# Scores on half the array's rows in banks shared with q, and the norm's factors by transposes

## The reference

```
scores = q @ k.T * 32**-0.5 + slope[h] * (j - i), masked to j <= i
out = softmax(scores) @ v; x = x + out @ Wout.T
```

```
qh = softmax over the head's 64 columns of Wq q; kh = softmax over the 1024 positions of Wk k
out = Wo (context(kh, vh) applied to qh) + bo
out = out / max(sqrt(sum over the 128 channels of out*out), 1e-12) * g * sqrt(128); x = x + out
```

## Time and profile before

| | us |
|---|---|
| median of three runs (lowest, highest) | 3303.05 (3302.89, 3307.04) |
| span of the profiled execution | 3299.9 |
| PE busy in the span | 3128.8 (95%) |
| DVE busy | 1773.3 (54%) |
| ACT busy | 1045.8 (32%) |
| POOL busy | 507.1 (15%) |

### The profile page before, as it was taken

How to read it: one execution, slowest core, us unless ns; L and a number is a source line. 1 busy time by engine, 2 the same in 40 slices (tenths; PEclk the granted TensorE clock), 3 DMA queues, 4 the chain that set the end, 5 groups by cost and what they waited for, 6 DMA issues and landing times. The chain is left out here.

```text
span 3299.9 us, 41826 instructions
## 1 busy us (share of the span) xinstructions
PE 3128.8 (95%) x15136; PEld 2393.9 (73%) x15136; DVE 1773.3 (54%) x2927; ACT 1045.8 (32%) x2356; POOL 507.1 (15%) x525
## 2 busy tenths in 40 slices
PE   7999997799999999999996799999999899999998
PEld 6888886566666666666663688888887788888887
DVE  5311112466666666666663655555555655555555
ACT  2100000566665566666651211111111211111111
POOL 2100000233333333333332100000000100000000
PEclk9999999899999999999996899999999999999999
DMA  4222223111111111111110432222122521231222
GB/s 144 93 73 75 73 70 116 41 39 38 43 46 51 38 38 39 50 38 51 38 33 31 129 82 55 76 65 75 54 82 76 153 64 54 81 81 54 62 74 78
DMA packets 83350, 218.73 MB, mean 66 GB/s; under 512 B 11984, under 2 KB 18256, under 8 KB 81232
## 3 DMA queue, kind: packets, MB, share of 16 engines
q1 hardware_dynamic: 83280, 217.78, 21.8%
HBM read 175.79 MB, written 41.94 MB: 66 GB/s over the span
## 5 line engine op out<-in xcount | busy, mean ns | idle before, releaser
L312 PE MATMUL ff_ps<-h_xT_hi,w_hi 128*128 128x512 f32 x1376 | 538.2, 391 | 13.2 <-DVE h_xT_lo L96 13.2
L312 PE MATMUL ff_ps<-h_xT_lo,w_hi 128*128 128x512 f32 x1376 | 537.1, 390 | 0.0
L312 PE MATMUL ff_ps<-h_xT_hi,w_lo 128*128 128x512 f32 x1376 | 537.0, 390 | 0.0
L1042 ACT ACTIVATE w_hi<-words 128x1024 fp32r<-128x1024 f32 x134 | 142.5, 1063 | 697.3 <-DVE words L1087 697.3
L1127 DVE TENSOR_TENSOR acc<-ff_po,acc 128x512 f32<-128x512 f32 x352 | 243.0, 692 | 210.6 <-PE ff_po L312 209.9
L312 PE MATMUL qkv_acc<-w_hi,xT_hi 128*128 128x512 f32 x768 | 300.9, 392 | 9.2 <-DVE w_lo L255 9.2
L312 PEld LDWEIGHTS ff_ps<-h_xT_hi,w_hi 128*128 128x128 f32 x1376 | 259.5, 189 | 68.3 <-issue 8.8
L312 PE MATMUL qkv_acc<-w_hi,xT_lo 128*128 128x512 f32 x768 | 299.4, 390 | 0.0
L312 PE MATMUL qkv_acc<-w_lo,xT_hi 128*128 128x512 f32 x768 | 299.3, 390 | 0.0
L312 PEld LDWEIGHTS ff_ps<-h_xT_hi,w_lo 128*128 128x128 f32 x1376 | 259.4, 189 | 54.1
L312 PEld LDWEIGHTS ff_ps<-h_xT_lo,w_hi 128*128 128x128 f32 x1376 | 259.6, 189 | 53.8
(11 more groups left out here) (156 smaller groups left out, 5305.9 us busy)
## 6 DMA issues: line engine op xcount, KB each, us to landing
words<-in_w SPq DMA_DIRECT2D x90, 512.0 KB, 3.5
qkv<-qkv_out SPq DMA_DIRECT2D x96, 256.0 KB, 2.0
words<-in_w SPq DMA_DIRECT2D x176, 128.0 KB, 4.0
sc<-in_s SPq DMA_DIRECT2D x88, 256.0 KB, 4.3
qk_in<-qkv SPq DMA_DIRECT2D x16, 1024.0 KB, 4.9
w_stage<-in_w_attn SPq DMA_DIRECT2D x56, 256.0 KB, 3.0
qkv_rows<-in_x SPq DMA_DIRECT2D x16, 512.0 KB, 3.8
ctx_in<-in_context SPq DMA_DIRECT2D x16, 512.0 KB, 3.7
```

The lines of the kernel that those rows point to most:

```text
L312: last = nc.tensor.matmul(out, left, right, start=n == 0, stop=n == len(pairs) - 1)
L1042: nc.scalar.activation(dst, src, ACT.Copy).then_inc(s["split_hi"], 1)
```

## The change

- The scores of a head group are two products of 64 rows and 256 columns: rows 0 to 63 hold heads 0 and 1, rows 64 to 127 heads 2 and 3. `kD` shrinks to two key blocks of 128 columns. The two results lie in two banks of PSUM, the first half of each bank of `pair_s`. DVE biases both with one instruction.
- `bank_s` and `bank_q` give way to `pair_s`: q is its bank 0, where half of the scores lie too; y is formed in both banks.
- PE's order in a step becomes s, P, AV, q, k, kt, m, d. s waits for q tile t-3 to be read, q for the scores of the same step to be biased.
- m tiles 2 and 3 go into `pair_k`; the third waits for all four copies of kT.
- The norm: each column of eight factors, repeated 128 times by a stride of nothing, is transposed into `bank_p` and `bank_d`. `diag`, its instruction and POOL's wait for it go.

```diff
-    kD = sb("kD", [P, G, HG, P], F32, ph)
+    kD = sb("kD", [P, G, 2, P], F32, ph)
...
+    pair_s = pb("pair_s", [P, 2, N], ph)
+    half_s = pair_s[:, :, 0:2 * P]
+    bank_q = pair_s[:, 0, :]
...
+    y_banks = [pair_s[:, e, :] for e in range(2)]
+    norm_banks = [bank_p, bank_d]
...
-    m_room = [pair_o[:, D - P:D]] * 2 + [bank_s[:, 0:P]] * 2
+    m_room = [pair_o[:, D - P:D]] * 2 + [pair_k[:, N:N + P], pair_k[:, 0:P]]
...
-            last = nc.vector.tensor_copy(kD[at, :, j, :], qkT[at, 1, :, :])
+            last = nc.vector.tensor_copy(kD[at, :, j % 2, :], qkT[at, 1, :, :])
...
+        by_half = [v.rearrange("p (a j) s -> p a (j s)", a=2) for v in (sc[:, t % SR, :, :],
+                                                                       bias[:, t * HG:(t + 1) * HG, :])]
+        nc.vector.scalar_tensor_tensor(by_half[0], half_s, float(HD) ** -0.5, by_half[1], ALU.mult, ALU.add).then_inc(
...
+            if own and t < G:
+                if t == 0:
+                    pe.wait_ge(s["a_out"], 2 * b + 2)
+                    pe.wait_ge(s["kd_out"], b + 1)
+                elif cross and t > 2:
+                    pe.wait_ge(s["q_subbed"], c * KT + t - 2)
+                else:
+                    pe.wait_ge(s["s_biased"], b * G + t)
+                for e in range(2):
+                    at = slice(e * 2 * HD, (e + 1) * 2 * HD)
+                    last = nc.tensor.matmul(half_s[:, e, :], qkT[at, 0, t, :], flat(kD[at, t, :, :]), start=True,
+                                            stop=True)
+                last.then_inc(s["s_done"], 1)
...
+            n = t - 2
+            if cross and 0 <= n < KT:
+                if n % 4 == 0:
+                    pe.wait_ge(s["x1_norm"], 2 * c + n // 4 + 1)
+                if own and t < G:
+                    pe.wait_ge(s["s_biased"], b * G + t + 1)
+                elif n:
+                    pe.wait_ge(s["q_subbed"], c * KT + n)
+                else:
+                    pe.wait_ge(s["y_scaled"], b)
+                nc.tensor.matmul(bank_q, xn[:, n * P:(n + 1) * P], wq_sb[:, 0, :], start=True,
+                                 stop=True).then_inc(s["q_done"], 1)
...
                 if i == 2:
-                    pe.wait_ge(s["s_biased"], (b + 1) * G)
+                    pe.wait_ge(s["kt_out"], (b + 1) * XT)
...
-            pe.wait_ge(s["n_diag"], c + 1)
-            for e, bank in enumerate(norm_banks):
-                last = nc.tensor.matmul(bank, ones[:, :], flat(diag[:, 4 * e:4 * e + 4, :]), start=True, stop=True)
+            pe.wait_ge(s["n_pow"], c + 1)
+            for k in range(KT):
+                last = nc.tensor.transpose(norm_banks[k // 4][:, k % 4, :],
+                                           n_sq[:, 1, k:k + 1].to_broadcast([P, P]), ident[:, :])
...
-            if cross:
-                pool.wait_ge(s["r_done"], b + 1)
...
-            dve.wait_ge(s["n_pow"], c + 1)
-            nc.vector.tensor_tensor(diag[:, :, :], ident[:, :].unsqueeze(1).to_broadcast([P, KT, P]),
-                                    n_sq[:, 1, :].unsqueeze(2).to_broadcast([P, KT, P]), ALU.mult).then_inc(s["n_diag"], 1)
```

More of the change, by code:

```diff
@@ L370, in attention_phase @@
     y_sq = kE
-    diag = xn[:, :].rearrange("p (a b) -> p a b", a=KT)
     n_sq = sb("n_sq", [P, 2, KT], F32, ph)
     neg8 = sb("neg8", [P, KT], F32, ph)
-    bank_s = pb("bank_s", [P, N], ph)
-    bank_q = pb("bank_q", [P, N], ph)
+    pair_s = pb("pair_s", [P, 2, N], ph)
+    half_s = pair_s[:, :, 0:2 * P]
+    bank_q = pair_s[:, 0, :]
     bank_p = pb("bank_p", [P, HG, P], ph)
@@ L380, in attention_phase @@
     pair_k = pb("pair_k", [P, 2 * N], ph)
-    norm_banks = [bank_q[:, :], flat(bank_d[:, :, :])]
-    turn4 = [bank_s[:, :].rearrange("p (a b) -> p a b", a=4), bank_q[:, :].rearrange("p (a b) -> p a b", a=4),
-             bank_p[:, :, :], bank_d[:, :, :]]
+    y_banks = [pair_s[:, e, :] for e in range(2)]
+    norm_banks = [bank_p, bank_d]
+    turn4 = [b.rearrange("p (a b) -> p a b", a=4) for b in y_banks] + [bank_p[:, :, :], bank_d[:, :, :]]
     names = ("qk_loaded v_loaded x_loaded ctx_loaded stored setup_in distances powers filled slopes masked gain w_in0 w_in1 w_in2 w_in3 w_hi_done w_lo_done "
@@ L390, in attention_phase @@
              "x_done x1_done x1_stats x1_aggr x1_mom x1_rstd x1_norm copied "
-             "y_done y_out y_squared y_gained n_done n_clamped n_pow n_diag r_done y_scaled fin").split()
+             "y_done y_out y_squared y_gained n_done n_clamped n_pow r_done y_scaled fin").split()
     s = {n: sem("a_" + n) for n in names}
@@ L480, in bias_scores @@
         dve.wait_ge(s["s_done"], b * G + t + 1)
-        nc.vector.scalar_tensor_tensor(flat(sc[:, t % SR, :, :]), bank_s[:, :], float(HD) ** -0.5,
-                                       flat(bias[:, t * HG:(t + 1) * HG, :]), ALU.mult, ALU.add).then_inc(
+        by_half = [v.rearrange("p (a j) s -> p a (j s)", a=2) for v in (sc[:, t % SR, :, :],
+                                                                       bias[:, t * HG:(t + 1) * HG, :])]
+        nc.vector.scalar_tensor_tensor(by_half[0], half_s, float(HD) ** -0.5, by_half[1], ALU.mult, ALU.add).then_inc(
             s["s_biased"], 1)
@@ L517, in turn_tensor @@
                     pe.wait_ge(s["p_out"], b * G + n)
+                elif cross:
+                    pe.wait_ge(s["y_scaled"], b)
                 for j in range(HG):
@@ L520, in turn_tensor @@
                 last.then_inc(s["p_done"], 1)
[L521 to L538, removed]
             n = t - 3
@@ L542, in turn_tensor @@
                     pe.wait_ge(s["v_loaded"], (b + 1) * 16)
+                    if cross:
+                        pe.wait_ge(s["x1_done"], 2 * b)
                 if n == G // 2:
@@ L570, in turn_tensor @@
                 if i == 2:
-                    pe.wait_ge(s["s_biased"], (b + 1) * G)
-                elif i:
+                    pe.wait_ge(s["kt_out"], (b + 1) * XT)
+                elif i == 1:
                     pe.wait_ge(s["m_out"], b * XT + i)
@@ L599, in turn_tensor @@
             pe.wait_ge(s["d_out"], (c + 1) * KT)
-            if own:
-                pe.wait_ge(s["s_biased"], (b + 1) * G)
-            for e, bank in enumerate((bank_s, bank_q)):
+            pe.wait_ge(s["q_subbed"], (c + 1) * KT)
+            for e, bank in enumerate(y_banks):
                 for j in range(XT):
-                    last = nc.tensor.matmul(bank[:, :], z[:, j, :], qT[:, j, e * N:(e + 1) * N], start=j == 0,
+                    last = nc.tensor.matmul(bank, z[:, j, :], qT[:, j, e * N:(e + 1) * N], start=j == 0,
                                             stop=j == XT - 1)
@@ L679, in turn_scalar @@
             act.wait_ge(s["y_done"], c + 1)
-            for e, bank in enumerate((bank_s, bank_q)):
-                last = nc.scalar.activation(y[:, e * N:(e + 1) * N], bank[:, :], ACT.Identity, bias=bo_sb[:, 0:1])
+            for e, bank in enumerate(y_banks):
+                last = nc.scalar.activation(y[:, e * N:(e + 1) * N], bank, ACT.Identity, bias=bo_sb[:, 0:1])
             last.then_inc(s["y_out"], 1)
@@ L748, in turn_vector @@
                 dve.wait_ge(s["q_done"], c * KT + n + 1)
-                nc.vector.tensor_reduce(q_max[:, n, :], bank_q[:, :].rearrange("p (h d) -> p h d", d=XD), AX.X,
+                nc.vector.tensor_reduce(q_max[:, n, :], bank_q.rearrange("p (h d) -> p h d", d=XD), AX.X,
                                         ALU.max).then_inc(s["q_maxed"], 1)
@@ L752, in turn_vector @@
                 nc.vector.tensor_tensor(qr[:, n % SR, :].rearrange("p (h d) -> p h d", d=XD),
-                                        bank_q[:, :].rearrange("p (h d) -> p h d", d=XD),
+                                        bank_q.rearrange("p (h d) -> p h d", d=XD),
                                         q_max[:, n, :].unsqueeze(2).to_broadcast([P, 8, XD]),
@@ L820, in turn_vector @@
             for e, bank in enumerate(norm_banks):
-                last = nc.vector.tensor_tensor(y[:, e * N:(e + 1) * N], y[:, e * N:(e + 1) * N], bank, ALU.mult)
+                last = nc.vector.tensor_tensor(y[:, e * N:(e + 1) * N], y[:, e * N:(e + 1) * N], flat(bank[:, :, :]), ALU.mult)
             last.then_inc(s["y_scaled"], 1)
```

## The result

The changed kernel takes 3338.05 us (median of 4 runs, 3336.33 to 3338.54) against 3302.97 of the kernel before beside it: ratio 1.0102, interval [1.0088, 1.0117]. Forecast were 3329 and "slower" with 0.82. The spans of the two profiled executions, 3336.5 and 3299.9, differ by 36.6.

A forecast was written before the change was run, and what follows sets the result against it. PE was taken to bound the kernel, busy 69.69 of a 72.70 us turn. Waits +37.7, norm -7.8, last turn -3.2 gave +26.7; with span 3299.9 and 3.15 kept, 3329.7, forecast as 3329, range 3300 to 3354.

The forecast's parts named there:

- Direction and mechanism: Attention turns: slower, chance 0.82, since q on PE waits for DVE's bias of the same step's scores; about 2.2 us a turn.
- Price of the halves: Scores on PE as two half-array products: X = 0.77 us, 0.09 less than now, between 0.43 and 1.20.
- Rival A: Scores: the half-array products are as good as free, X = 0.43; +1.5 us a turn, total 3315; chance 0.17.
- kt0 to k1: Turn's start, first key transposes to the start of k1: 4.78 us becomes 5.10, +0.32, reckoned at half clock.
- k's end to kt in steps 5 and 7: From the end of k2 or k3 to the next key transposes: 3.04 us becomes 3.59, +0.55 each.
- kt3 to the third m: Last key transposes to the third m tile, which now waits for the fourth copy of kT: 3.15 us becomes 3.4, +0.3.
- The norm: Eight transposes replace two products, 0.86 us less on PE; next turn's first steps come 0.56 sooner, 14 turns, -7.8.
- The last turn: Norm in the last turn, all exposed: 5.17 us from the diagonal's start to the scaling shrinks, -3.2.
- Rival B: Waits let PE's clock fall once more a turn: +24 us, 3354; chance 0.15 together with halves running one after the other.
- a growth in their number: Sign of being wrong: PE's half-clock stretches grow in number.
- Rival C: q's wait for the bias costs nothing if DVE's chain from k's end takes under 2.1 us, not 2.73: 3282; chance 0.13.

The follow-up runs named there:

- bias edit: The changed kernel with one DVE instruction moved, the bias of the scores ahead of the sum of q in each step: 3311.37 us, ratio 1.0023.
- kernel with full rows: The changed kernel with scores again one product of 128 rows, in the bank shared with q, all waits kept: 3334.34 us, ratio 1.009.

## Why the prediction was right, point by point

- **Direction and mechanism**: right. q's wait for the bias costs in steps 3, 5 and 7, and in step 2 too, DVE's chain of maximum, sum and bias fills it, and PE's savings ahead of it are swallowed. The bias edit shows the first, with the start of a turn where q has its own bank, and the kernel with full rows the second.
- **Price of the halves**, X = 0.77 taken from AV's switching: measured 0.78 in step 5. That it fits so closely is partly luck: AV's rows give 0.32 for the switching and not 0.34 (no row shows the "longer weight load"), and in steps 2 and 3 the pair saves nothing against 0.86. Rival A (0.43), and with it the span model of the Trainium skill's page "TensorE: Matmul & The Clock Gate", Part 3, is refuted for this pair of f32 products: its four passes take 0.64 from the first start to the next group's, where two passes of 256 columns would stream in 0.21 each. What the Trainium skill's page "TensorEngine Tiling (Array Packing)", Key Properties, says, that a change of mode drains the engine, agrees with the 0.09 ahead of s.
- **kt0 to k1**: mis-sized, +0.88 for +0.32. The term was worked out in a turn with a slow stretch. Eight of 15 turns run this piece at full clock after the change (ten before), and there the wait of 0.75 is bare; in the seven with a slow stretch the view shows no wait of q in step 2 at all. This is the largest miss: 0.56 by 15 turns, 8 us, with the slow stretches reckoned apart.
- **k's end to kt in steps 5 and 7**: 0.65 for 0.55. The wait is 2.74 for 2.73, but q behind it takes 0.96, not 0.86. So it does in step 2, behind the pause with no AV ahead (889.87 to 890.83), and behind AV with no pause; which of the two adds the 0.1 is open.
- **kt3 to the third m**: +0.59 for +0.3, place and releaser right. kT's copy stands in ACT's queue behind the exponential of q, and q's reads on DVE now come after the late q; ACT's timeline shows the pause that I had left out, and the copy ends 4.7 after the last bias, not 4.31:

```profile
919.88 0.63 ACT L674 ACTIVATE qr<-qr 128x512 f32<-128x512 f32 x1 [0.27 <-DVE qr L762]
920.41 0.58 ACT L678 ACTIVATE qT<-bank_d 128x512 f32<-128x512 f32 x1
920.89 1.02 ACT L681 ACTIVATE kT<-pair_k 128x1024 f32<-128x1024 f32 x1
```

- **The norm**: -0.85 for -0.56 a turn. I held that the diagonal's going is worth nothing beyond PE's time. It is worth something: DVE's timeline after shows the residual (L804) waiting for PE, where it had come late behind the diagonal and the key blocks, and the scaling (L828) directly behind the moments.

```profile
879.55 0.69 DVE L804 TENSOR_TENSOR x<-pair_o,x 128x512 f32<-128x512 f32 x1 [2.55 <-PE pair_o L312]
881.32 0.14 DVE L823 TENSOR_SCALAR x_mom<-x_mom 128x1 f32<-128x1 f32 x1
881.38 0.68 DVE L828 TENSOR_TENSOR v_in<-v_in,bank_p 128x512 f32<-128x512 f32 x1
```

  From the moments' last row to the scaling 0.06, before 0.74; from z's products to the residual 22.80 for 22.96.
- **The last turn**: -3.2, as forecast. With the norm alone it was 0.5, with other slow stretches in that turn.
- The misses partly cancel: +15 from the pieces, -5 from the norm and the turn that leads out of the first; the span grew by 36.6 for the 26.7 forecast, and what lies around it was 1.6 less than I had kept (3.15 set one execution's span beside the median of others; each run's own time is 1.8 above its own span), so the time came 8 to 9 beyond the forecast. That these cancel is luck.
- **Rival B** (one more slow stretch a turn): did not come; seven stretches for five, the same cost in all. But I had named a growth in their number as a sign of being wrong, and it grew. That it cost nothing was not foreseen: a single stretch adds 1.53 to a turn before and 0.6 to 0.85 after. **Rival C** (the wait is covered): did not come, but its condition was the right one: with DVE's chain shorter by 0.66 most of the wait goes.

## What to carry to other kernels

Before two results are put into one PSUM bank, follow the reader of the first through its own queue: the wait costs what stands ahead of that read, here a maximum and a sum on DVE (2.74 us for 0.68 of bias), there four exponentials on ACT. A wait moved to where an engine must stand also swallows what was saved ahead of it, so price savings behind the wait, not in front. Where two parts of a change are independent, run each alone: the norm by transposes gives 3286 (0.9945), faster than both kernels. And where a repair brings a wait of its own, compare the pieces of a turn and not the totals: q in its own bank saved only 6 us in all, yet its first two pieces show what the shared bank had cost.

## What the hardware showed that I had not expected

- With the same 2.11 gap per turn and the same work up to k1, TensorE gets a slow stretch at 0.50 of the clock in five of 15 turns (before) or in two (norm alone). In the kernel before one stretch adds 1.53 to a turn; after, 0.6 to 0.85, with q's wait of 0.75 gone from those turns, and 2.0 where it is about twice as long (a mean granted clock of 0.96 over the turn for 0.98). A difference of a few us between two kernels of this kind can be that alone.
- An idle time in brackets understates what the pause costs PE: with 0.56 in brackets q started 0.63 after AV's columns had ended, and taking a wait of 0.41 away gave back 0.68.
